# A state-space layer with a mixture of experts on one core: state 11 moves from the transposing path to the row path on VectorE, and every engine's order of work is rewritten

## The reference

```python
xn = layernorm(x)                        # x: [16, 256, 256]
x + mamba(xn) + moe(xn)
# mamba: E = 512 channels, N = 16 states, T = 256 tokens
hidden, gate = split(xn @ W_in);  u = silu(conv4(hidden) + bias)
dt_low, B, C = split(u @ W_x);    dt = softplus(dt_low @ W_dt + b_dt)
for t: state = exp(dt * A) * state + dt * B * u;  y = sum_n state_n * C_n
(y + u * D) * silu(gate) @ W_out
# moe: 32 experts, top 8 of a softmax, each silu(x @ wg) * (x @ wu) @ wd, 96 wide
```

## Time and profile before

| | us |
|---|---|
| median of 3 runs | 1347.76 (1347.3 to 1347.85) |
| the profiled execution | 1342.44 |
| its span | 1340.6 |
| PE, DVE, ACT, POOL busy | 1301.6, 1239.6, 1213.2, 1233.9 |

### The profile page before, as it was taken

One profiled execution on the slowest core, in us unless ns is written; L12 is line 12 of the kernel. 1 busy time (PEld: TensorE's weight loads), 2 busy tenths in 40 slices (PEclk: granted clock), 3 DMA queues, 4 the chain that ended last, 5 costly groups with the idle time before them and its releaser, 6 DMA issues.

```text
span 1340.6 us, 26644 instructions
## 1 busy us (share of the span) xinstructions
PE 1301.6 (97%) x9222; PEld 1219.6 (91%) x9222; DVE 1239.6 (92%) x1644; ACT 1213.2 (90%) x2111; POOL 1233.9 (92%) x674
## 2 busy tenths in 40 slices
PE   6899999999999999999999999999999999999998
PEld 5889999999999999999999999999999899999987
DVE  3799999999999999999999999999999999999997
ACT  5879999999999999999999999999999899999984
POOL 2999999999999989999999999989999999999996
PEclk9999999999999999999999999999999999999999
DMA  7543443544444344443544444344443534434342
GB/s 193 160 144 118 143 120 115 152 115 132 139 127 135 112 136 127 139 120 118 149 120 126 136 128 138 114 132 131 139 122 116 148 114 134 139 113 142 109 146 80
DMA packets 189399, 174.95 MB, mean 130 GB/s; under 512 B 43185, under 2 KB 172241, under 8 KB 189265
## 3 DMA queue, kind: packets, MB, share of 16 engines
q1 hardware_dynamic: 150864, 121.86, 30.5%
q10 hardware_dynamic: 38400, 51.40, 13.6%
HBM read 167.92 MB, written 5.24 MB: 129 GB/s over the span
## 4 chain that ended last, share of the span: by engine, by line
POOL 27%; issue 21%; ACT 19%; DVE 18%; PE 12%; DMA 2%; ACTq 1%; SPq 0%; DVEq 0%; POOLq 0%
POOL state L571 14%; POOL moe L586 6%; ACT decay L657 5%; PE pair_ps L1003 5%; ACT L657 5%; ACT L665 4%; DVE state L878 4%; PE out_ps L1138 3%; POOL state L580 3%; DVE dt L865 3%; DVE u L891 2%; DVE decay L878 2%; DVE u L919 2%; ACT moe L665 2%; DVE moe L898 2%
## 5 line engine op out<-in xcount | busy, mean ns | idle before, releaser
L571 POOL TENSOR_TENSOR state<-du,b_rep 128x1024 f32<-128x1024 f32 x256 | 611.7, 2395 | 61.1 <-DVE u L891 59.3
L878 DVE TENSOR_TENSOR_SCAN state<-decay,state 128x512 f32<-128x512 f32 x448 | 534.2, 1212 | 21.1 <-ACT decay L657 16.4
L657 ACT ACTIVATE decay<-dt,neg_a 128x255 f32<-128x255 f32 x1024 | 436.7, 465 | 37.7 <-DVE state L878 19.0
L1138 PE MATMUL out_ps<-w_down,moe 128*128 128x256 f32 x1536 | 355.9, 381 | 3.1 <-POOL moe L586 1.9
L1138 PEld LDWEIGHTS out_ps<-w_down,moe 128*128 128x128 f32 x1536 | 282.5, 190 | 38.6 <-issue 4.1
L586 POOL TENSOR_TENSOR moe<-moe,rw_rep 128x512 f32<-128x512 f32 x192 | 249.3, 1309 | 8.7 <-DVE moe L898 7.3
L580 POOL TENSOR_TENSOR state<-state,c_rep 128x1024 f32<-128x1024 f32 x96 | 244.1, 2543 | 1.6 <-DVE state L878 1.6
L1003 PE MATMUL pair_ps<-xnT_hi,w_gate_hi 128*128 128x256 f32 x768 | 228.9, 298 | 3.2 <-DVE moe L898 3.2
L1003 PE MATMUL pair_ps<-xnT_hi,w_up_hi 128*128 128x256 f32 x768 | 225.7, 294 | 2.8 <-ACT moe L665 1.9
L657 ACT ACT_TABLE_LOAD x171 | 219.4, 1283 | 2.5
L1003 PE MATMUL pair_ps<-xnT_lo,w_gate_hi 128*128 128x256 f32 x768 | 216.4, 282 | 0.0
(11 more groups left out here) (149 smaller groups left out, 2252.5 us busy)
## 6 DMA issues: line engine op xcount, KB each, us to landing
w_down<-in_L_ffn_w_down_dram SPq DMA_DIRECT2D x384, 128.0 KB, 2.9
b_rep<-b_dram ACTq DMA_DIRECT2D x128, 256.0 KB, 3.3
rw_rep<-rw_dram SPq DMA_DIRECT2D x256, 96.0 KB, 2.7
c_rep<-b_dram ACTq DMA_DIRECT2D x128, 128.0 KB, 3.3
rw_rep<-rw_dram SPq DMA_DIRECT2D x256, 64.0 KB, 2.6
rw_rep<-rw_dram SPq DMA_DIRECT2D x256, 32.0 KB, 2.6
x_in<-L_attn_input_states_dram SPq DMA_DIRECT2D x16, 256.0 KB, 3.8
res<-L_attn_input_states_dram SPq DMA_DIRECT2D x16, 256.0 KB, 3.1
```

The costliest lines, as they stand in the source:

```text
L571: pool.tensor_tensor(state[:, n % STATES, :, :], du2[:, q, :, :], b_rep[:, n // BCH % 2, n % BCH, :][:, None, :].broadcast_to([P, ET, T]), ...
L657: last = act.activation(decay[:, h, j, 1:T], dt[:, q, e, 1:T], ACT.Exp, scale=neg_a[:, e, n:n + 1])
L878: dve.tensor_tensor_scan(a if n in ROWS_BY_VECTOR else x, a, x, 0.0, ALU.mult, ALU.add).then_inc(scanned, 1)
L1138: last = pe.matmul(out_ps[:, c, :], moe[:, p % RING, j, c * P:(c + 1) * P], w_down[:, p % RING, j, :], start=(p == 0 and j == 0 and c == 0 ...
```

## The change

State 11 joins `BY_ROW` and `ROWS_BY_VECTOR`: nine states are rows, three of them (5, 9, 11) on VectorE alone. Seven states are left to the transposing path. `gated` waits for the gate's SiLU as well. All order tables are replaced. The middle blocks' rows of those that the text speaks of, and the first block's warm-up:

```diff
-    BY_ROW = [n for n in range(NS) if n in ((2, 4, 5, 6, 8, 9, 10, 12))]
+    BY_ROW = [n for n in range(NS) if n in ((2, 4, 5, 6, 8, 9, 10, 11, 12))]
...
-               [-1, 12, 28, 39, 43, 55, 62, 71, 96, 97, 117, 120],
+               [-2, 12, 37, 38, 46, 52, 69, 70, 96, 99, 117, 120],
...
-    GATE_SILU_AT = [[54, 64], [63, 68], [74, 189]]
+    GATE_SILU_AT = [[52, 70], [55, 69], [64, 233]]
...
-              [14, 23, 41, 46, 59, 63, 79, 92, 107, 108, 127, 129],
+              [12, 23, 46, 50, 60, 63, 83, 90, 104, 109, 126, 129],
...
-    ROW_ADD_AT = [... [37, 49, [44, 47], 61, 78, [76, 76], 102, 119], ...
+    ROW_ADD_AT = [... [36, 50, [45, 45], 61, 79, [77, 78], 100, [90, 94], 116], ...
...
-                [17, 29, 37, 44, 65, 66, 80, 91, 99, 103, 131, 133],
+                [18, 31, 39, 41, 52, 71, 73, 84, 103, 106, 134, 135],
...
-    ROW_MUL_AT = [... [21, 32, [43, 45], 55, 67, [72, 76], 90, 92], ...
+    ROW_MUL_AT = [... [18, 28, [44, 45], 42, 70, [73, 77], 74, [90, 92], 89], ...
...
-    C_LOAD_AT = [... [-10, -10, 26, 40, 41, 61, 70, 80], ...
+    C_LOAD_AT = [... [-17, 1, 23, 45, 47, 53, 73, 76, 86], ...
...
-    ROWS_BY_VECTOR = [n for n in BY_ROW if n in ((5, 9))]
+    ROWS_BY_VECTOR = [n for n in BY_ROW if n in ((5, 9, 11))]
...
-    WARM_AT = [[-119, 4], [-59, 15], [1, 50], [14, 7], [24, 6]]
+    WARM_AT = [[-86, 17], [-26, 11], [-12, 7], [3, 15], [7, 19], [28, 5]]
...
             def gated(i, q):
 
+                pool.wait_ge(gate_read, 2 * i + 2)
                 pool.wait_ge(y_summed, 2 * i + 2)
```

More of the change, by code:

```diff
@@ L86, in build @@
[L86 to L92, removed]
@@ new lines, in build @@
+    OUT_AT = [[31, 41, 42, 59, 64, 70, 85, 93, 105, 124, 145, 148],
+              [37, 45, 51, 62, 64, 84, 89, 103, 114, 122, 141, 145],
+              [46, 64, 84, 96, 135, 139, 149, 180, 188, 198, 232, 239]]
+    TURN_AT = [[[3, 3], [7, 21], [29, 40], [68, 68], [110, 114], [121, 123], [128, 132]],
+               [[12, 12], [17, 19], [31, 31], [73, 75], [109, 113], [118, 121], [124, 129]],
+               [[8, 9], [15, 23], [44, 49], [112, 118], [186, 192], [194, 204], [210, 210]]]
+    TURN_Y_AT, PROJECT_AT = [[139, 139], [133, 135], [227, 231]], [159, 159, 243]
@@ new lines, in build @@
+    PE_FRONT = [{'xnT': -109, 'hid0': -100, 'hid1': -98, 'logits': -89, 'weightsT': -26, 'low': -86, 'lowT': -63, 'dt0': -48, 'dt1': -46},
+                {'xnT': -116, 'hid0': -105, 'hid1': -96, 'logits': -80, 'weightsT': -57, 'low': -47, 'lowT': -43, 'dt0': -39, 'dt1': -23},
+                {'xnT': -116, 'hid0': -101, 'hid1': -94, 'logits': -83, 'weightsT': -51, 'low': -48, 'lowT': -42, 'dt0': -38, 'dt1': -23}]
+    GATE_AT = [[55, 59], [51, 59], [89, 172]]
+    SILU_AT = [[-80, -12, 20, 30, 39, 46, 69, 70, 84, 86, 108, 109],
+               [-2, 12, 37, 38, 46, 52, 69, 70, 96, 99, 117, 120],
+               [-4, 11, 29, 37, 44, 45, 64, 69, 84, 87, 156, 222]]
@@ new lines, in build @@
+    SCALAR_FRONT = [{'xnT': -123, 'hid0': -120, 'hid1': -118, 'weightsT': 1, 'low': -90, 'lowT': -73, 'dt0': -58, 'dt1': -36},
+                    {'xnT': -113, 'hid0': -108, 'hid1': -94, 'weightsT': -55, 'low': -48, 'lowT': -41, 'dt0': -38, 'dt1': -23},
+                    {'xnT': -114, 'hid0': -107, 'hid1': -95, 'weightsT': -56, 'low': -45, 'lowT': -41, 'dt0': -36, 'dt1': -26}]
+    SCALAR_ALONE = [{'conv_silu': -102, 'router_exp': -73, 'softplus': -18, 'first_state': 12, 'skip': -8, 'normed': -125, 'share': -18},
+                    {'conv_silu': -74, 'router_exp': -77, 'softplus': -19, 'first_state': 7, 'skip': 22, 'normed': -124, 'share': -66},
+                    {'conv_silu': -59, 'router_exp': -79, 'softplus': -19, 'first_state': 6, 'skip': -7, 'normed': -123, 'share': -68}]
@@ new lines, in build @@
+    GATE_SILU_AT = [[52, 70], [55, 69], [64, 233]]
+    MUL_AT = [[-14, 12, 34, 42, 48, 57, 77, 81, 94, 105, 118, 127],
+              [12, 23, 46, 50, 60, 63, 83, 90, 104, 109, 126, 129],
+              [12, 17, 43, 46, 52, 66, 78, 79, 94, 108, 159, 180]]
+    ADD_AT = [[[16, 26], [34, 63], [82, 99], [114, 117], [119, 119], [130, 130]],
+              [[20, 23], [63, 78], [98, 109], [113, 114], [117, 125], [127, 131]],
+              [[17, 33], [47, 48], [75, 79], [113, 127], [141, 147], [161, 173]]]
@@ new lines, in build @@
+    SUM_AT = [[135, 136], [133, 134], [218, 235]]
+    WEIGH_AT = [[14, 30, 31, 36, 40, 54, 72, 72, 88, 110, 133, 133],
+                [18, 31, 39, 41, 52, 71, 73, 84, 103, 106, 134, 135],
+                [21, 28, 35, 38, 61, 62, 68, 88, 97, 147, 173, 198]]
+    ROW_MUL_AT = [[20, 32, [40, 44], 45, 59, [72, 77], 79, [91, 93], 110], [18, 28, [44, 45], 42, 70, [73, 77], 74, [90, 92], 89], [23, 30, [42, 45], 55, 68, [72, 77], 76, [88, 95], 149]]
+    POOL_ALONE = [{'rstd': -90, 'step_input': -21, 'gated': 141, 'select': -35},
+                  {'rstd': -128, 'step_input': -17, 'gated': 137, 'select': -78},
+                  {'rstd': -128, 'step_input': -20, 'gated': 250, 'select': -79}]
```

46 lines of the change are left out of this document (11 added, 35 removed).

## The result

The changed kernel takes 1339.12 us, median of 20 runs (1336.61 to 1343.67), the kernel before 1346.22 on the same chip (20 runs, 1341.55 to 1347.99). The ratio is 0.9957, 95% interval 0.9946 to 0.9968: **faster, by some 5.8 us by the ratio (7.1 between the medians) where 14.2 were forecast**. The runs of the kernel before lie in two groups, near 1342.5 and near 1347.5 us (beside the experiments, where its clock is on record, at a granted clock of 0.997 to 1.000 and of 0.995 to 0.997), and its profiled one belongs to the lower. So the two profiled spans are only 2.6 us apart (1340.6 and 1338.0), and times by stretch are compared between these two. What the medians differ by beyond that is in no trace.

The account below looks back on a forecast made before the run. TensorE and GpSimd were taken as tied bounds; 0.9 us a block, 14 us, was let pass. The profiled 1342.44 us becomes 1328.2, and 5.3 us up to the median gives 1333.5 us, range 1319 to 1352.

Parts of the forecast that it names:

- the sum: All engines: TensorE and GpSimd tied, 0.9 us a block passes, 14 us in all, giving 1333.5 us.
- part 1: TensorE: state 11 no longer transposed, 0.89 us a block, 14.2 us in all, on the path.
- part 7: Start and end, with the first and last blocks and the clock: nought, 3 us either way.
- Part 2: VectorE: two additions go, two products and two half sums come; +1.3 us a block, 20 us, within its idle time.
- part 5: Order of row sums and GpSimd's products: nought for GpSimd within 0.9 us either way, 1 us for VectorE.
- Part 3: ScalarE: 291 table loads, 72 us less, at most +0.7 us a block of new work; no gain counted directly.
- rival B: VectorE becomes the bound as every row sum meets an operation: 80.1 to 81.0 us a block, 1343 to 1356; chance 0.22.
- Part 6: ScalarE's queue of loads of C: the load for state 12 waits for GpSimd's product of state 10; hidden, no cost.
- The signs: Whole kernel: right if period near 79.5, 291 table loads, 896 transposes; wrong if period above 80.2 or below 78.8.
- A: GpSimd's idle waits become stretches and ScalarE's relief helps: 1.6 to 2.5 us a block, 1311 to 1324; chance 0.14.
- C: GpSimd's product of state 10 comes late for scan 12, so slower: 1355 to 1369; chance 0.10.
- D: New order fails: requests meet GpSimd as before, SiLUs wait for TensorE; part of 0.9 us passes, 1340 to 1350; chance 0.08.

Follow-up runs that it names:

- the orders alone: Changed kernel with state 11 back on TensorE's transposes, one addition of state 7 earlier and the last block in its old order: 1351.36 us, ratio 1.0056 to the kernel before.
- the loads put back: Changed kernel with two small SiLUs among the decays of states 3 and 7, four table loads more a block: 1435.57 us, ratio 1.0676 to the kernel before.

## Why the prediction was right in sign and wrong in size

**The step that failed** is the sum: "TensorE gets 0.9 us ... I let 0.9 us a block pass", which rests on part 1's "this lies on the path while TensorE is the fullest engine". That was read from a busy share. Two runs show it to be wrong: 5.6 us a block less on TensorE moved the kernel before by 0.1 us at a full clock, and the new orders with the transposes kept have the changed kernel's 79.80. The second step that failed is "I take nought" for the start and the end, which cost 5.2 us (part 7).

The chain of waits within one middle block of the kernel before could have said so. Start, us, what; some of the longer pieces from 779 to 860 us:

```profile
787.47 2.34 POOL state L580
791.16 1.28 ACT L665
793.07 1.28 ACT L657
...
808.48 1.28 ACT L665
...
811.34 1.28 ACT L657
...
823.98 1.24 DVE u L891
...
828.98 2.33 POOL state L571
```

None of the 115 longest pieces in that stretch is TensorE's. The chain goes through GpSimd, ScalarE with its table loads, VectorE and GpSimd again. Ten of the 13 middle periods are like this one; in the other three, which take 80.60 to 80.70 us, 41 us of the chain are TensorE's. The same stretch of the changed kernel:

```profile
784.00 3.45 PE out_ps L1149 x16
...
815.79 2.84 PE pair_ps L1004 x24
...
818.85 0.89 PE turn_ps L1101 x8
819.80 2.70 POOL state L571
...
842.95 1.16 POOL du L554
...
854.76 1.10 ACT x_in L712 x2
...
855.99 0.63 PE front_ps L1018 x4
```

Here TensorE leads without a gap to 819.8, then GpSimd to the norm, ScalarE and TensorE again. So in this block the chain moved from ScalarE and VectorE to TensorE and GpSimd; it does so in six of the 13 periods. At least two loops of about 79.8 us are tied in the changed kernel, one with TensorE in it and one nearly without, and since no engine is busy all of a period, each passes through more than one. The cuts, each run once, agree: one engine lighter gives 0.1 us at most, GpSimd and VectorE together 0.4, with far more off GpSimd 0.9. Which loop binds in each experiment was not worked out.

*Part 1.* Removed as said, 896 transposes stand; worth nothing in a middle block, since the orders with these transposes have the same 79.80. Adding their 0.89 us to the limit of at most 78.9 gives at most 79.8, so with them TensorE could be one of the tied loops. The chain of the orders alone agrees: 40 to 54 us of it are TensorE's in 12 of the 13 middle periods, in place of 44 us in six. So the saving has begun to free TensorE; what it frees is not worth time while the other loop stands.

*Part 2.* VectorE's busy time rose by 17 us in the long stretch, where 20 of work and 16 of longer row sums were the terms. The work came; the sums did not grow (part 5).

*Part 3.* The 291 loads are right but for one. Of the 72 us, 66.5 show in ScalarE's busy time from 80 to 1220 us. VectorE's waits for decays fell from 32.9 us to 14.9 (14.4 and 0.5), under the 20 forecast; of that 1.1 us a block at most 0.6 can be in the period. The Trainium skill (ScalarE: Activation LUTs, What ACT_TABLE_LOAD costs) adds a drain to each load. A ScalarE 149 us lighter would be that; the fall of 66.5 us in busy time is no more than the loads' own 1283 ns, and no drain shows in it. Nor does one show in the loads put back, where four cost 4.9 to 5.3 us at a full clock.

*Part 5.* I took nought for GpSimd, from bounds of 0.9 either way, and 1 us more for VectorE. All three sums that GpSimd stood idle for became stretches, which alone is the lower bound. Two of the three held operations of one block, behind sums that begin at 711.26 and 739.74 us:

```profile
711.42 3.26 POOL L580 TENSOR_TENSOR state<-state,c_rep 128x1024 f32<-128x1024 f32 x1 [0.90 <-DVE state L879]
...
740.03 3.17 POOL L571 TENSOR_TENSOR state<-du,b_rep 128x1024 f32<-128x1024 f32 x1 [0.18 <-PE turn_ps L1101]
```

The third is a weighing of 2.13 us for 1.28. With the new waits for scans, GpSimd's balance is the 0.6 us of the section on the result. VectorE's 1 us did not come: the mean row sum didn't rise, as part 5 and rival B had it, but fell, 1479 ns (L892 above) for 1552. The three sums above still take 1.20 to 1.23 us, as they begin in a short gap ahead of the operation that they hold, and the block's other three take 1.73, 1.33 and 2.03 us where they took 2.05, 1.44 and 2.19. The Trainium skill (SBUF — State Buffer, SBUF: two separate sides) calls the shared ports an exclusive lock; the longer products (2689 ns in the mean, 2543 before) agree. The orders carry the gain, and this is the largest change in them that the traces show; its 0.9 us bound holds the 0.6 found. That it is this term and not the table loads in the chain isn't shown: no run takes either alone out of the kernel before.

*Part 6.* Costed at nothing, which holds: in the trace the load of state 11's row lands just in time, and the product waits 0.22 us for it:

```profile
661.74 0.34 ACTq L644 DMA_DIRECT2D c_rep<-b_dram  x1
...
665.76 0.70 DVE L913 TENSOR_TENSOR decay<-decay,c_rep 128x512 f32<-128x512 f32 x1 [0.22 <-DMA c_rep<-b_dram]
...
667.26 0.38 ACT L687 ACTIVATE low_tok<-front_ps 128x256 f32<-128x256 f32 x1 [1.78 <-POOL state L580]
```

What I didn't see is that low_tok stands behind the next load; moving the load shows that it costs nothing.

*Part 7.* "I take nought, and 3 us either way" for start and end together: they cost 5.2 us, 2.4 and 2.8. That is the larger part of the miss. Of the 14.2 us forecast, the profiled executions show 2.6: the 13 middle periods gave 7.8 where 13 x 0.9 = 11.7 were due, and the ends took 5.2 where some 2.5 were due. What in the ends costs this is open.

*The median.* The sum adds 5.3 us to come from the profiled execution to the median of three runs, 1347.76. Over 20 runs that median is 1346.22, so 1.5 us of this term did not hold.

*The signs.* Those named for "right" came nearly all: 292 table loads, 896 transposes, 14.9 us of waits for decays, 6.1 us of idle time before state inputs. The period of 79.80 is 0.3 above the 79.5 named and below the 80.2 that was to show the forecast wrong. None of them asks whether TensorE's time is on the path, nor about the ends, so they could come with both steps wrong.

*Rivals.* A didn't come: less than TensorE's share fell, though its idle waits did turn into stretches. B's mark, a mean row sum over 1.9 us, is absent; VectorE is at 96.4%. C is absent: VectorE waits for GpSimd's inputs 7.1 us in all, 14 of the 16 times for at most 0.4 us, as the 0.37 us ahead of the scan of state 9 at 654.07 us. D's outcome, only part of the 0.9 us, is what came, though 1339.12 lies just under its 1340 to 1350 and just inside the forecast's 1325 to 1340. Its mark is absent: the requests do meet GpSimd otherwise, 2.5 us of waits for 59.3. A median close to the forecast's edge is partly luck, as the kernel before came out 1.5 us faster over 20 runs than the sum had it.

## What to carry to other kernels

An engine's high busy share is no proof that its freed time comes back: follow the chain of waits through one middle block first, and if the engine isn't in it, price its cut at nought until the others are loosened as well. A place in the chain is no proof either: TensorE leads the changed kernel's for 40 us in six of 13 blocks, and a cut inside that stretch gave nothing. Before a cut is said to test a chain, check that what it takes out stands in it. Where four engines lie within a few per cent, test the limits by cutting two engines at once; single cuts on one or the other showed nothing here. Compare periods at the same granted clock, block by block. With orders written out by hand, price the first and last block by themselves, for they ate two thirds of what thirteen middle blocks had gained.

## What was not expected

- **TensorE's granted clock fell when its work was cut.** With 5.6 us a block off TensorE in the kernel before the clock went from 0.999 to 0.986 and the time up by 0.45%; the blocks at 0.98 are 0.6 us longer than those at 1.00. At 2.8 us off in the changed kernel it was 0.989 with the first half of the block cut and 0.997 with the second.
- **The place of a table load decides its price.** Four more among the decays of the changed kernel cost 4.9 to 5.3 us a block at a full clock; four less, outside the chain, gave nothing in the kernel before.
- **GpSimd's order is worth 10 us a block** (90.05 us for 79.80, at a clock of 0.970) with no operation added or removed.
